# Attention stage of a four-layer ViT tower: scores and class values as four 32-column products side by side, contexts turned and the class row summed two products later

## The reference, cut to what matters

```
B, S, D = x.shape            # 8, 513, 256
qkv = (x @ W_qkv + b_qkv).reshape(B, S, 3, H, hd)      # H = 16, hd = 16
q, k, v = (qkv[:, :, 0], qkv[:, :, 1], qkv[:, :, 2])
attn = jnp.einsum('bqhd,bkhd->bhqk', q, k) / jnp.sqrt(jnp.asarray(hd, x.dtype))
attn = jax.nn.softmax(attn, axis=-1)
attn_out = jnp.einsum('bhqk,bkhd->bqhd', attn, v).reshape(B, S, D)
...
return attn_out + moe_out
```

## Time and profile before

| | |
|---|---|
| median of three runs | 2006.7 us (2005.04 to 2009.29) |
| the profiled execution | 2004.92 us, of which the span is 2003.2 us |
| busy in the span | PE 91%, DVE 74%, POOL 48%, ACT 47% |
| softmax attention | from about 1575 us to the end |
| granted TensorE clock there | 1.00 of full speed (2.4 GHz) |

### The profile page before, as it was taken

One profiled execution on the slowest core, in us unless ns is written; L12 is line 12 of the kernel. 1 busy time (PEld: TensorE's weight loads), 2 busy tenths in 40 slices (PEclk: granted clock), 3 DMA queues, 4 the chain that ended last, 5 costly groups with the idle time before them and its releaser, 6 DMA issues. The chain is left out here.

```text
span 2003.2 us, 36356 instructions
## 1 busy us (share of the span) xinstructions
PE 1831.2 (91%) x10746; PEld 1205.2 (60%) x10746; DVE 1482.6 (74%) x4076; ACT 939.3 (47%) x2132; POOL 963.7 (48%) x1654
## 2 busy tenths in 40 slices
PE   6997997999899999899999699599889699999997
PEld 5886774444688888677777433288767333333332
DVE  3334896777477777699998388667789699999991
ACT  1112564566122122344444244345544488777777
POOL 3554564566333433233333111068844576666664
PEclk9997998999799999999999799699989799999999
DMA  4331568797100000597000200047877444444420
GB/s 135 115 115 32 151 177 202 159 181 153 48 1 1 1 1 1 215 414 292 1 1 1 64 9 11 27 122 200 207 227 232 99 100 105 107 97 95 94 70 28
DMA packets 241706, 215.01 MB, mean 107 GB/s; under 512 B 117210, under 2 KB 216188, under 8 KB 241404
## 3 DMA queue, kind: packets, MB, share of 16 engines
q1 hardware_dynamic: 227804, 183.51, 34.2%
q0 software_dynamic: 9408, 25.70, 4.1%
q10 hardware_dynamic: 4320, 3.70, 0.7%
HBM read 108.04 MB, written 103.12 MB: 105 GB/s over the span
## 5 line engine op out<-in xcount | busy, mean ns | idle before, releaser
L2932 ACT ACTIVATE attend_w<-ps 128x512 f32<-128x512 f32 x512 | 280.0, 598 | 78.0 <-PE ps L2792 71.2
L3160 DVE TENSOR_REDUCE attend_mx<-ps 128x1 f32<-128x512 f32 x448 | 281.8, 681 | 33.0 <-PE ps L2780 31.6
L2792 PE MATMUL ps<-keep_o,keep_x 99*128 99x512 bf16 x512 | 191.1, 382 | 9.3 <-DMA keep_o<-attend_nparts 6.9
L2780 PE MATMUL ps<-keep_x,keep_o 96*128 96x512 bf16 x448 | 172.6, 385 | 1.9 <-DVE attend_mx L3160 0.2
L987 POOL TENSOR_TENSOR keep_early<-keep_early,first_causal 128x128 f32<-128x128 f32 x256 | 111.2, 458 | 77.8 <-ACT keep_early L961 76.8
L1009 DVE SCALAR_TENSOR_TENSOR keep_early<-ps,first_causal 128x512 f32<-128x512 f32 (+3 forms) x256 | 111.3, 485 | 45.4 <-PE ps L901 44.5
L1215 PE MATMUL ps<-mlp_zT,keep_early 128*128 128x128 f32 x1056 | 128.5, 281 | 8.0 <-ACT mlp_zT L1257 8.0
L2810 PE MATMUL ps<-attend_w,keep_early 128*17 128x512 f32 x1024 | 135.5, 598 | 0.0
L961 ACT ACTIVATE keep_early<-ps 128x512 f32<-128x512 f32 (+3 forms) x256 | 97.0, 435 | 75.1 <-PE ps L901 74.6
L1215 PEld LDWEIGHTS ps<-mlp_zT,keep_early 128*128 128x128 f32 x1056 | 122.2, 194 | 16.0 <-ACT mlp_zT L1257 16.0
L2780 PEld LDWEIGHTS ps<-keep_x,keep_o 96*128 96x128 bf16 x448 | 43.7, 98 | 134.4 <-DVE attend_mx L3160 95.4
(11 more groups left out here) (409 smaller groups left out, 4488.7 us busy)
## 6 DMA issues: line engine op xcount, KB each, us to landing
sorted<-keep_x SPq DMA_DIRECT2D x3, 14720.0 KB, 75.1
tok_xin<-in_xk SPq DMA_DIRECT2D x64, 256.0 KB, 2.6
qk_parts<-qkv_parts SPq DMA_DIRECT2D x33, 384.0 KB, 3.2
qk_parts<-moe_parts SPq DMA_DIRECT2D x32, 384.0 KB
sorted<-moe_zn POOLq DMA_DIRECT2D x64, 128.0 KB, 3.0
moe_zs<-sorted SPq DMA_DIRECT2D x45, 128.0 KB, 3.0
keep_o<-qk_parts SPq DMA_DIRECT2D x14, 384.0 KB, 4.5
keep_x<-qk_parts SPq DMA_DIRECT2D x14, 384.0 KB, 5.7
```

What stands on the lines that cost most here:

```text
L2780: nc.tensor.matmul(ps[:, bank, :], qs[0:R, x.buf(0), h, t * P:(t + 1) * P], ks[0:R, x.buf(0), h, :], start=True, stop=True).then_inc(s_msc, 1)
L2792: nc.tensor.matmul(ps[:, SC + i % RING, :], ks[:, x.buf(2), HG * g + j, kt * P:(kt + 1) * P], qs[:, x.buf(2), HG * g + j, :], start=True, ...
L2932: nc.scalar.activation(w[:, j, kt % 2, :], ps[:, SC + (HG * k + j) % RING, :], ACT.Exp)\
L3160: nc.vector.tensor_reduce(mx[:, t, k:k + 1], ps[:, MX + (at + 1) % RING, :], AX, ALU.max)\
```

## The change

`product` issues four matmuls where one stood: the loaded operand's 128 columns are cut into four times 32, and each goes to its own quarter of the array, with the same streamed operand. It serves `max_scores`, `scores`, and in the same form `class_values`. `pT` loses its padding, so that L2848 gives 8 columns of output, and the column sum L2860 uses one column of ones. In steps 6 and 7 side work moves from j = 1 to j = 3, just ahead of `values`. DVE no longer clears the padding of `pT`.

```diff
+            def product(bank, keys, queries):
+
+                for q in range(P // QUAD):
+                    cols = slice(QUAD * q, QUAD * (q + 1))
+                    last = nc.tensor.matmul(ps[cols, bank, :], keys[:, cols], queries, start=True, stop=True,
+                                            skip_group_check=True, tile_position=(0, QUAD * q))
+                return last
...
-                nc.tensor.matmul(ps[:, bank, :], qs[0:R, x.buf(0), h, t * P:(t + 1) * P], ks[0:R, x.buf(0), h, :],
-                                 start=True, stop=True).then_inc(s_msc, 1)
+                product(bank, qs[0:R, x.buf(0), h, t * P:(t + 1) * P], ks[0:R, x.buf(0), h, :]).then_inc(s_msc, 1)
...
-                nc.tensor.matmul(ps[:, SC + i % RING, :], ks[:, x.buf(2), HG * g + j, kt * P:(kt + 1) * P],
-                                 qs[:, x.buf(2), HG * g + j, :], start=True, stop=True).then_inc(s_sc[j], 1)
+                product(SC + i % RING, ks[:, x.buf(2), HG * g + j, kt * P:(kt + 1) * P], qs[:, x.buf(2), HG * g + j, :])\
+                    .then_inc(s_sc[j], 1)
...
-                    nc.tensor.matmul(ps[:, CTX, :], vb[:, b, half, 2 * HD * HG * g:2 * HD * HG * (g + 1)],
-                                     cwp[:, half, :], start=True, stop=False, skip_group_check=True)
+                    for q in range(P // QUAD):
+                        cols = slice(QUAD * q, QUAD * (q + 1))
+                        nc.tensor.matmul(ps[cols, CTX, :], vb[:, b, half, 2 * HD * HG * g + QUAD * q:2 * HD * HG * g + QUAD * (q + 1)],
+                                         cwp[:, half, :], start=True, stop=False, skip_group_check=True, tile_position=(0, QUAD * q))
...
-                        last = nc.tensor.matmul(ps[:, MISC, 0:VW], pT[:, t, :, :].rearrange("p a h -> p (a h)"), v[:, x.buf(1), t, :],
+                        last = nc.tensor.matmul(ps[0:HALF, MISC, 0:VW], pT[:, t, :], v[:, x.buf(1), t, :],
...
-                nc.tensor.matmul(ps[:, MISC, 0:VW], env.ones[:, :], t1[:, 1, :, :].rearrange("h g d -> h (g d)"),
+                nc.tensor.matmul(ps[0:1, MISC, 0:VW], env.ones[:, 0:1], t1[:, 1, :, :].rearrange("h g d -> h (g d)"),
...
-                        if j == (2 if k % TB == 1 else 1):
+                        if j == (2 if k % TB == 1 else 3 if k > STEPS - 3 else 1):
                             side_work(x, k)
...
-            nc.vector.memset(pT[:, :, :, :], 0.0)
```

More of the change, by code:

```diff
@@ L2646, in pass_attend @@
     SC, MX, CTX, MISC = 0, RING, 2 * RING, 2 * RING + 1
+    QUAD = 2 * HD
     with a.ctx:
@@ L2667, in pass_attend @@
         pc = a.sb("pc", [HALF, S])
-        pT = a.sb("pT", [P, TB, P // HALF, HALF])
+        pT = a.sb("pT", [P, TB, HALF])
         t1 = a.sb("t1", [P, 2, HALF, HD + 1])
@@ L2938, in _ @@
                         past(act, s_C, c)
-                        nc.scalar.copy(pT[:, :, 0, :], ps[:, MISC, 0:TB * HALF].rearrange("p (t h) -> p t h", h=HALF))\
+                        nc.scalar.copy(pT[:, :, :], ps[:, MISC, 0:TB * HALF].rearrange("p (t h) -> p t h", h=HALF))\
                             .then_inc(s_PT, 1)
```

## The result

The changed kernel takes 2050.4 us (median of 4 runs, 2047.8 to 2056.1) against 2006.0 us before (four runs as well, one more than in the table ahead); the ratio is 1.022, with a 95% interval from 1.0195 to 1.0249. It is slower, though the interval leaves open whether by 2%, and the forecast of 1998.5 us (1985 to 2013) was wrong. The profiled execution has a span of 2046.2 us, 43.0 us more than before.

A forecast was written before the change was run, and what follows sets the result against it. PE was taken to set the pace, 26.45 us a slot. Terms of -0.46 us per slot times 14 gave -6.5, the last two slots -1.5, together -8 us: 1998.5 us forecast, range 1985 to 2013.

The forecast's parts named there:

- the price of a product in quarters: Scores and class terms on PE: four matmuls for one still cost 0.22 us, no change; ends -0.3 and +0.9 us per slot.
- No transfer is added: Data movement in the attention stage: the change adds no transfer, and POOL's addition of contexts comes at most 0.9 us later.
- The signs that were to show it: In the new profile: wrong if quarter products' starts follow more slowly than 59 ns, or loads wait with nothing to wait for.
- The slower rival: Issue becomes PE's bound, a product costing over 0.236 us (59 ns a pair); about 2019 us at 0.25; chance 0.18.
- `values` saves both edges: Passage into and out of `values` on PE: 8 a slot lose 0.21 us each, 1.7 us less per slot.
- The transposes pay 0.2 us each: Transposes of steps 1, 2 and 6 stay 128 wide: new edges of 0.09 + 0.11 us, 0.6 us per slot.
- Class contexts and class sum free of edges: Steps 5 and 7, now 8 and 1 columns: no edge cost; at the other end 0.2 us each, 0.4 per slot.
- ACT's wait at the small transposes of step 4: PE waits about 0.36 us there for ACT's class-token exponentials, allowing 0.12 us from ACT's end to PE's start.
- DVE at the start of a slot: Maxima from step 6 into the next slot: DVE gains 0.24 us where PE counted 0.42, so 0.18 us lost to waits.
- The third wait: Step 5: class term and contexts wait for ACT's copies, which follow a `values`; 0.1 us, up to 0.2.
- The sum of -0.46 us per slot: Attention slot: PE's own -1.1 us plus waits of 0.36, 0.18 and 0.1; times 14 slots, -6.5 us.
- The forecast of the time: Whole kernel: -8 us, profiled execution from 2004.9 to 1996.9, shown median 1.8 higher, so 1998.5 us.

The follow-up runs named there:

- e13: Kernel before, each product cut into four matmuls along the queries, each over all 128 output columns, gathers where they were: 2065.5 us, ratio 1.030.
- e12: Changed kernel with GpSimd's work laid apart as in e9, turn and class sum two products earlier, at their old places: 2000.7 us, ratio 0.9973.
- e14: e12 with class contexts and class sum over 128 columns again: 2008.0 us, ratio 1.0012.
- e15: e12 with the small transposes of step 4 one pair of products later: 1997.7 us, ratio 0.9961.
- e9: Changed kernel with gathers spread one at a time and GpSimd's combinings held back from DVE's small operations: 2004.1 us, ratio 0.9988.
- e10: Kernel before with GpSimd's work laid apart in the same way as e9: 2004.6 us, ratio 0.9990.
- e11: Changed kernel with each indirect gather replaced by a plain load of 128 neighbouring rows at the same place: 2002.9 us, ratio 0.9981.
- e4: Changed kernel with the four indirect gathers of a slot issued after GpSimd's combining, about 10 us later: 2068.6 us, ratio 1.035.
- e3: Changed kernel with class contexts computed four times, in 8 columns of each quarter, only the first read: 2064.6 us, ratio 1.028.
- e1: Changed kernel with the class contexts of step 5 put back to all 128 output columns: 2064.6 us, ratio 1.028.
- e5: Changed kernel without its indirect gathers from the second slot on (58 of 66 left out): 2014.2 us, ratio 1.0038.
- e6: Kernel before with the same 58 indirect gathers left out as in e5: 2013.6 us, ratio 1.0041.
- e7: Changed kernel with all gathers kept, but spread one by one between GpSimd's other pieces of work: 2015.0 us, ratio 1.0044.

## Why the prediction was wrong

**The step that failed** is the price of a product in quarters: "I take 0.22, no change", bounded from above by issue alone ("From above it is issue that counts"). Both bounds were of the starts of matmuls, and those held, 0.22 us for a product. What the step left out, at nothing and without a reason, is the other end: a reader has to wait until four matmuls are reported done, where it was one. (The semaphore is raised once for a product, as before, so it is not the semaphore updates that became more.) While GpSimd's indirect gathers run, about 5 us of each slot, PE's reports go out at about one matmul in 0.19 us. A whole product each 0.22 us just passes; four matmuls in 0.22 us pile up, the readers are 1.2 to 3.4 us late, the three banks of each kind are used up, PE stands for some 2.5 us and then works at half clock in step 6, 1.3 us more. A slot lasts 29.6 us instead of 26.1. That the gathers do it is shown by four runs (moved, left out, spread, plain), that it goes by the number of matmuls by e13. What in a gather holds the reports stays open.

**The sentence beside it**, "No transfer is added", is true, but it let the transfers that were there drop out of the reckoning: one of them turned from harmless to decisive. The trace of before had a sign of it, which I took no account of (timelines of PE and DVE, at the gathers of that slot):

```profile
1734.75 0.38 PE L2780 MATMUL ps<-keep_x,keep_o 96*128 96x512 bf16 x1
...
1735.49 1.29 DVE L3160 TENSOR_REDUCE attend_mx<-ps 128x1 f32<-128x512 f32 x2 [0.23 <-PE ps L2780]
```

The product, behind the four matmuls of the turn, ends at 1735.13, and DVE, idle from 1735.27, starts on it at 1735.49, 0.36 us behind its end. Just as the first gather begins (1729.78), DVE, idle as well, starts at 1729.88 on a product that ends at 1729.84. PE had another bank to fill, so it cost nothing there.

**The signs that were to show it.** Starts of quarter matmuls did not follow more slowly than 59 ns a pair: 0.22 us for four. Loads did wait with nothing to wait for, the other sign of being wrong: 52.7 us of "issue" at `product` from 1640 to 1990 us. But e12, which has no stall, has 38.3 us of it from 1640 to 1902, as much for its time. That sign could not tell the two apart.

**The slower rival** had the right sign by the wrong mechanism. It saw issue as the bound; four quarter matmuls in 0.22 us are 55 ns for a pair, under its break-even of 59 ns. They are also under the 62 ns that the Trainium skill, TensorE: Matmul & The Clock Gate, section "Wait — 56ns, not 53.3ns?", gives where hardware decode is off. This trace doesn't show that page's bound.

**The other terms**, seen where the hold is out of the way:

- `values` saves both edges: right (0.22 us ahead, 0.86 for itself).
- The transposes pay 0.2 us each: too little. The way in costs 0.32 us against 0.22, the rest 0.59 against 0.43: 0.26 us, and for three jobs 0.8 us a slot instead of 0.6.
- Class contexts and class sum free of edges: right, 0.40 us a slot between e12 and e14.
- ACT's wait at the small transposes of step 4, 0.36 us: 0.30, and on the path by e15. The 0.12 us allowed from ACT's end to PE's start stood without a row; it is 0.14 in the changed kernel (1738.70 to 1738.84).
- DVE at the start of a slot, 0.18 us: 0.25 a slot in e9, 0.29 in e12. The third wait, 0.1 us: none named for PE.
- The sum of -0.46 us per slot: -0.33 in e9 and -0.36 in e12, from 26.45. The measured terms give the same: -1.7 + 0.8 + 0.30 + 0.25 = -0.35. Against the ten even slots of e10 it is less, 26.33 to 26.10 us in the same stretch of e9.
- The forecast of the time: 8 us less than 2006.7 is 1998.7, not 1998.5. Without the stall the change gains less than that: e9, the change with GpSimd in another order, takes 2004.1 us, e10, the kernel before in that order, 2004.6, and e11, the change with plain loads, 2002.9.

So the mechanism that the prediction weighed was right in kind and near in size in the slots, though in e9 too small to be seen in the whole time, and one that it didn't look for cost 3.5 us a slot (29.6 against 26.1), more than seven times the sum.

The Trainium skill says of the rows themselves, Perfetto Trace Analysis, section "Tensor Engine Instruction (MATMUL, LD_WEIGHTS)", that a matmul's end in a profile is computed, and that its semaphore goes out only when PSUM has acknowledged all bytes. This trace has a gap that leaves room for it: the modelled end of the product started at 1743.04 is 1743.76, its reader starts at 1747.19. What lies between is seen in the readers alone, so whether the matmul itself, its write or the news of it was late is not shown. Nor is it shown that the hold is there without a profiler: every run on record has a span and a granted clock from a recording.

## What to carry to other kernels

When one matmul becomes four, count what has to be reported done as well as the starts, and look for stretches where reports are already late: an idle reader beside a matmul that has ended, with a releaser that makes no sense, is that sign. Move or spread the gathers of GpSimd before cutting matmuls beside them, or keep whole matmuls there. When a work queue is reordered, check again what its long operations lie beside.

## What the runs showed of the hardware

- While GpSimd ran indirect gathers, TensorE's products were reported at about one matmul in 0.19 us (0.73 to 0.75 us for four, in the changed kernel, e4 and e13; once, in e4, 1.40 us for four), from at most 1.9 us after the first gather's start (in e4 an idle ScalarE gets the scores of 1732.81 at 1734.20) to about 1 us after the last one's end (1736.05 and 1737.10). Plain loads on the same queue with the same bytes did not do this. Whether the making of the descriptors or the scattered rows is behind it was not tried.
- TensorE's own starts can stop too, with no releaser named: 18.1 us in 400 us of e3 and 7.3 in e1, against 0.5 in 350 us of the changed kernel.
- Narrow matmuls in one quarter let the other quarters of later products start first, by 0.34 us (1743.04 and 1743.38). By itself this cost nothing measurable (e5, e14).
- Beside GpSimd's multiplication of 1.05 us, DVE's small operations between SBUF tiles take 1.07 or 1.56 us instead of 0.35. The Trainium skill, SBUF — State Buffer, section "SBUF: two separate sides", says that the two share a port pair that one instruction holds to its end. The trace agrees for the operation of 1.07 us: it starts 0.18 us behind the multiplication (1737.36 and 1737.18) and ends 0.20 us behind its end (1738.43 and 1738.23). That of 1.56 us starts ahead of the multiplication, beside a gather, and ends 0.16 us behind it (1685.34 and 1685.18). Such operations took 1.2 to 1.3 us a slot from VectorE in e5, e6 and e7, in other places each time, and 0.5 in the kernel before.
